# Layer 1's attention stream: another order of VectorE's and ScalarE's work in the slots, and the rows to route turned ahead of the tile's mixing

## The reference

```python
x = x + tanh(g_xattn[0]) * L0_xattn(layernorm(x), ctx)   # attention both ways, gated
x = x + tanh(g_ffn[0])   * L0_ffn(layernorm(x))          # 8 experts, the 4 best per token
x = x + tanh(g_xattn[1]) * L1_xattn(layernorm(x), ctx)
x = x + tanh(g_ffn[1])   * L1_ffn(layernorm(x))          # 8 experts, the 2 best per token
```

```python
queries, keys, values = x @ Wq.T + bq, ctx @ Wk.T + bk, ctx @ Wv.T + bv
attn = softmax(queries @ keys.T / 16)
out = (x + attn @ values) @ Wo.T + bo
gate_logits = y @ gate_w + gate_b           # y: layernorm of the stream after attention
topk_vals, topk_idx = top_k(gate_logits, 2)  # softmax over the two gives the weights
```

## Time and profile before

| what | us |
|---|---|
| median of three runs (1516.46 to 1520.41) | 1517.4 |
| the profiled execution's own time | 1517.85 |
| its span | 1516.0 |
| layer 0's attention and routing, 0 to about 500 | 500 |
| layer 0's experts, to about 927 | 427 |
| layer 1's attention stream, about 927 to 1220 | 293 |
| layer 1's last routing and experts, to the end | 296 |
| TensorE busy over the span | 1400.1 (92%) |
| VectorE busy | 790.1 (52%) |
| ScalarE busy | 736.8 (49%) |
| GpSimd busy | 504.6 (33%) |

### The profile page before, as it was taken

How to read it: one execution, slowest core, us unless ns; L and a number is a source line. 1 busy time by engine, 2 the same in 40 slices (tenths; PEclk the granted TensorE clock), 3 DMA queues, 4 the chain that set the end, 5 groups by cost and what they waited for, 6 DMA issues and landing times. The chain is left out here.

```text
span 1516.0 us, 25943 instructions
## 1 busy us (share of the span) xinstructions
PE 1400.1 (92%) x10086; PEld 1281.0 (84%) x10086; DVE 790.1 (52%) x1658; ACT 736.8 (49%) x1399; POOL 504.6 (33%) x389
## 2 busy tenths in 40 slices
PE   5799989999998999999999999999989889999997
PEld 5686966967855899999999898998979769899996
DVE  3545666666656353554454233465665775455421
ACT  3344454454443465555565454454442435666653
POOL 1200100101011664665565443131211125667643
PEclk8899999999999999999999999999998979999999
DMA  4302022021113453553553234031202145555332
GB/s 135 126 12 70 29 75 71 15 87 59 43 52 101 118 144 53 145 148 61 121 152 61 53 54 119 1 109 51 76 32 85 30 155 155 128 132 154 66 52 37
DMA packets 73680, 127.57 MB, mean 84 GB/s; under 512 B 7952, under 2 KB 53664, under 8 KB 73504
## 3 DMA queue, kind: packets, MB, share of 16 engines
q1 hardware_dynamic: 46816, 81.92, 16.4%
q0 software_dynamic: 26688, 43.34, 15.0%
HBM read 100.44 MB, written 24.79 MB: 83 GB/s over the span
## 5 line engine op out<-in xcount | busy, mean ns | idle before, releaser
L2425 DVE TENSOR_TENSOR m_hidden_lo<-m_act_out,m_hidden_hi 128x512 fp32r<-128x512 f32 x224 | 155.0, 692 | 363.2 <-ACT m_hidden_hi L2367 324.2
L420 PE MATMUL banks<-m_down_hi,m_hidden_hi 128*128 128x256 f32 x896 | 258.6, 289 | 4.1 <-DVE m_hidden_lo L2425 3.4
L420 PE MATMUL banks<-m_down_lo,m_hidden_hi 128*128 128x256 f32 x896 | 254.9, 284 | 2.9 <-issue 2.9
L420 PE MATMUL banks<-m_down_hi,m_hidden_lo 128*128 128x256 f32 x896 | 254.8, 284 | 0.0
L420 PE MATMUL banks<-m_xt_hi,m_up_hi 128*128 128x256 f32 x640 | 185.6, 290 | 3.3 <-DVE m_xt_lo L2408 3.3
L420 PE MATMUL banks<-m_xt_hi,m_up_lo 128*128 128x256 f32 x640 | 182.0, 284 | 0.0
L420 PE MATMUL banks<-m_xt_lo,m_up_hi 128*128 128x256 f32 x640 | 182.0, 284 | 0.0
L420 PEld LDWEIGHTS banks<-m_down_hi,m_hidden_hi 128*128 128x128 f32 x896 | 171.1, 191 | 8.9 <-DVE m_hidden_lo L2425 4.9
L420 PEld LDWEIGHTS banks<-m_down_lo,m_hidden_hi 128*128 128x128 f32 x896 | 171.2, 191 | 3.3 <-issue 3.3
L420 PEld LDWEIGHTS banks<-m_down_hi,m_hidden_lo 128*128 128x128 f32 x896 | 171.0, 191 | 0.0
L2504 POOL DMA_INDIRECT m_other_block<-rows,list_i x84 | 91.3, 1087 | 162.8 <-DVE list_i L1495 99.7
(11 more groups left out here) (367 smaller groups left out, 3568.5 us busy)
## 6 DMA issues: line engine op xcount, KB each, us to landing
stage<-in_down SPq DMA_DIRECT2D x22, 512.0 KB
stage<-in_ctx_cols SPq DMA_DIRECT2D x26, 402.0 KB
stage<-in_ctx_rows SPq DMA_DIRECT2D x20, 512.0 KB
stage<-in_up SPq DMA_DIRECT2D x20, 512.0 KB
m_stage<-in_up SPq DMA_DIRECT2D x11, 512.0 KB
m_stage<-in_down SPq DMA_DIRECT2D x10, 512.0 KB
rows<-xn SPq DMA_DIRECT2D x8, 528.0 KB, 3.4
stage<-in_ctx_picked SPq DMA_DIRECT2D x8, 512.0 KB
```

The costliest lines, as they stand in the source:

```text
L420: mm = q.e.matmul(dst, a, b, start=first and n == 0, stop=last and n == 2, skip_group_check=True)
L2425: q.e.tensor_tensor(lo, m.act[(n * HP + h) % ACTS], f32(hi), ALU.subtract).then_inc(*hidden_lo.mark((layer, n, h)))
```

## The change

It has five parts, all in layer 1's stream.

1. `who`: the low parts of the context's columns of batches 1 to 3 all go to DVE (two more pieces of 128x804 in slots 3, 7 and 11; POOL does two fewer). Rows are split as before.
2. `vector_attention_1`: the statistics of batch b+2 (`norm_in`) move from the end of slot i = 3 to slot i = 2, ahead of the queries' low parts. The two marks of slot i = 2 move to the next slot, ahead of `vector_scores`. In slot i = 3 the two puts stand ahead of the columns.
3. `mix_first`: in slots 8, 9, 12, 13, 16 and 17 `turned_lo` stands ahead of `vector_scores`.
4. TensorE turns the rows to route ahead of the mixing in slots 6, 10 and 14. ScalarE makes xn at the start of these slots, right behind the probabilities' high parts, and `a_routed_hi` ahead of `a_mixed`.
5. `vector_place` is cut in two; in the last batch its first instruction, which reads the bank, stands at the end of slot 16 and not in slot 17.

```diff
@@ who
-                return ("a", "pd"[n[2] % 2]) if n[0] else ("a", "d")
+                return ("a", "p" if kind == "cr" and n[2] % 2 == 0 else "d") if n[0] else ("a", "d")
@@ tensor_attention_1
+                if b and i == 2:
+                    tensor_turn_x(q, "r", 1, b - 1)
                 if 1 <= t <= LAST:
                     tensor_mix(q, 1, *of_tile(t - 1))
-                if b and i == 2:
-                    tensor_turn_x(q, "r", 1, b - 1)
@@ scalar_attention_1
                 if 1 <= t <= LAST:
                     scalar_turn_probs(q, 1, *of_tile(t - 1))
+                if b and i == 2:
+                    scalar_apply(q, "out", 1, b - 1)
...
-                elif i == 2:
-                    if b:
-                        scalar_apply(q, "out", 1, b - 1)
-                    if more:
-                        scalar_queries(q, 1, b + 1)
+                elif i == 2 and more:
+                    scalar_queries(q, 1, b + 1)
...
+                if b and i == 2:
+                    scalar_turn_x(q, "r", 1, b - 1)
                 if 1 <= t <= LAST:
                     scalar_mix(q, 1, *of_tile(t - 1))
...
-                if b and i == 2:
-                    scalar_turn_x(q, "r", 1, b - 1)
@@ vector_attention_1
+                if 2 <= b < BATCH and i == 3:
+                    vector_mark(q, 1, b - 2, 0)
+                    vector_mark(q, 1, b - 2, 1)
+
+                mix_first = b >= 2 and i < 2
+                if mix_first:
+                    vector_turn_mix(q, 1, *of_tile(t - 2))
                 if t < LAST:
                     vector_scores(q, 1, b, i)
-                if t >= 2:
+                if t >= 2 and not mix_first:
                     vector_turn_mix(q, 1, *of_tile(t - 2))
...
-                        vector_place(q, 1, b - 2)
+                        vector_place_parts(q, 1, b - 2)
...
                 elif i == 2:
+                    if b + 2 < BATCH:
+                        vector_measure(q, "in", 1, b + 2)
                     if more:
                         vector_queries(q, 1, b + 1)
-                    if b >= 2:
-                        vector_mark(q, 1, b - 2, 0)
-                        vector_mark(q, 1, b - 2, 1)
                 elif i == 3:
                     if more:
                         vector_bias(q, 1, b + 1)
-                        convert(q, "d", columns_of(b + 1))
                     if b >= 2:
                         vector_put(q, 1, b - 2, 0)
                         vector_put(q, 1, b - 2, 1)
+                    convert(q, "d", columns_of(b + 1))
+                    if b >= 2:
                         vector_mark(q, 1, b - 2, 2)
                         vector_mark(q, 1, b - 2, 3)
-                    if b + 2 < BATCH:
-                        vector_measure(q, "in", 1, b + 2)
...
                 if t == LAST:
                     vector_weigh(q, 1, b - 2)
+                    vector_place_number(q, 1, b - 2)
```

6 lines of the change are left out of this document (5 added, 1 removed).

## The result

| | us |
|---|---|
| before, median of 4 runs (1516.43 to 1520.41) | 1516.9 |
| after, median of 4 runs (1488.21 to 1495.64) | 1491.5 |
| ratio, with its 95% interval | 0.983 [0.980, 0.986] |
| the profiled execution of after; its span | 1495.64; 1493.8 |
| forecast; its range | 1499.0; 1491 to 1511 |

What follows compares the result with a forecast made beforehand. TensorE sets the pace, so its waits and its clock in layer 1's stream can be won: 9.7 us of waits plus 8.75 of clock, 18.45, give 1499.4 us (1499.0 against the median), range 1491 to 1511.

Steps and rivals of the forecast that it cites:

- reaches the end: The question whether the stream's gain reaches the kernel's end; behind the stream the experts are TensorE's too.
- The sum of waits: TensorE's waits in layer 1's stream, summed over slots: 9.7 us won.
- tail, slots 4 and 8: TensorE's waits for the low part of the probabilities' tail, 1.9 us twice, both go: +3.8 us.
- slot 6: Routed rows' turning: the wait of 1.28 us gives way to a new bank wait of 2.6 us: -1.3 us.
- slot 10: Routed rows' turning ahead of the mixing: a wait of 3.67 us becomes 2.6 us: +1.1 us.
- slot 14: No queries here, the bank comes free with the probabilities' low parts and xn is ready in time: +2.0 us.
- slot 9: The output's gain from an earlier `turned_lo` is given back at VectorE's first `a_x`: 0 us.
- bank wait at the second half of L684: Slots 6 and 10: TensorE waits 2.6 us for a bank that `a_cols_lo` of the queries' first half frees.
- rival (d): Slower: the columns on VectorE stay at 2.4 us each, the kernel takes 1524 us; chance 0.06.
- The clock: Falls of TensorE's clock behind waits that go are won back: 8.75 us, bounds -1.7 to 13.9.
- Rival (b): The clock comes back in full, no new fall: 23.6 us won, 1494.3; chance 0.16 shared with another rival.
- rival (a): The clock doesn't come back, falls stay where tiny products and a short wait meet: 8.0 us, 1509.9; chance 0.18.

Runs made afterwards that it cites:

- e1: The kernel before with parts 1 and 2 alone (columns' low parts all on VectorE, statistics, marks and puts moved): ratio 0.987 to before.
- e5: The changed kernel without part 4, the routed rows turned behind the mixing again: ratio 0.985 to before, stream 237.4 us.
- e10: The changed kernel measured once more with no further edit, in another set: ratio 0.983 to before, median 1488.3 us.
- e2: The kernel before with part 4 alone, the routed rows turned ahead of the mixing: ratio 0.996 to before.
- e3: The kernel before with part 3 alone, `turned_lo` ahead of the greatest score in slots 8, 9, 12 and 13: ratio 0.995 to before.
- e4: The kernel before with idle products ahead of slot 12's choosing and slot 13's output, no work moved: ratio 0.997 to before.
- e6: The changed kernel without part 3, `turned_lo` behind the greatest score again: ratio 0.989 to before.
- e7: The changed kernel with half of the columns' low parts back on GpSimd: ratio 0.989 to before.
- e12: The changed kernel with queries' high parts ahead of the exponential (slots 6, 10), plus reorderings around slots 5, 9, 13, 14 and 17: ratio 0.981 to before.
- e9: The kernel before with idle products at seven places of slots 4 to 14 where TensorE waited, no work moved: ratio 0.999 to before.

## Why the prediction was right or wrong

**What bounds the kernel: right.** TensorE's waits and its clock, in the stream, are where the 25.2 us come from, and behind the stream the time is the same. That isn't quite the forecast's "reaches the end": TensorE stands 3.2 us longer there, and the clock happens to lose 3.8 less. Of the 25.2 us 0.9 are slot 1's fall, which is chance.

**The sum of waits, 9.7 forecast, was about right.** By the profile it is 11.4 in the stream; 1.6 of it are given back behind the stream's end, which leaves 9.8. By the average of the remainder it is 12.1 (3.0). Point by point, from the earlier trace rows and their answers:

| term | forecast | measured |
|---|---|---|
| tail, slots 4 and 8 | +3.8 | 1.89 + 1.87 to 0: +3.8 |
| lists | +0.9 | 0.92 to 0.24: +0.7 |
| slot 6 | -1.3 | 1.28 to 2.23: -0.95 |
| slot 10 | +1.1 | 3.67 to 2.22: +1.45 |
| slot 14 | +2.0 | 1.49 + 0.49 to 0.90: +1.1 |
| slot 13 | +1.3 | 2.52 to 0.97: +1.55 |
| slot 9 | 0 | 2.53 to 0.98 + 1.06: +0.5 |
| slot 12 | +1.7 | 2.15 to under 0.3: +1.9 |
| place | +0.2 | 1.51 gone, L1547 for `a_x` 0.45 to 2.01: -0.05 |

The bank wait at the second half of L684 exists, at the place named, and is 2.2 and not 2.6 us. TensorE, ScalarE and VectorE in after, slot 6:

```profile
1030.94 0.60 PE L684 MATMUL banks<-small,xn 128*128 128x128 f32 x4
```

```profile
1032.15 0.20 ACT L927 ACTIVATION_READ_ACCUMULATOR a_probs<-banks,nbias 128x1 f32 x1
```

```profile
1032.96 1.41 DVE L557 SCALAR_TENSOR_TENSOR a_cols_lo<-banks,fold_cols,a_cols_hi 128x512 fp32r<-128x512 f32 x2 [0.24 <-ACT a_cols_hi L550]
```

The exponential ends at 1032.35, 0.8 us behind the first four transposes (forecast 0.96), and the bank is free 1.4 us later, at 1033.77 (forecast 1.65). The columns' 0.99 us held, so rival (d) didn't come. That `xn` would be ready in slot 14 was wrong by 0.9 us. Slot 9's gain did come back at `a_x` as the prediction says, but not quite all.

**One term had the right size under the wrong name.** Slot 10 was booked on part 4. e1 shows that moving the marks takes the wait from 3.67 to 1.28, with the turning where it was, and e5 that with the other parts in part 4 wins nothing measurable. Terms of a sum that meet at one wait can't be added without asking what the wait is once the other part is in.

**The clock, 8.75 forecast, is the step that failed.** It gave 13.9 by TensorE's busy time and 13.5 (3.0) on average over the runs, the upper bound of the prediction's range (13.9). Of the whole miss of 7 us this is about 5; the rest is the waits' term (12.1 on average against 9.7). The step that failed reads: half of 3.55 comes back in slot 10, a new fall of 1.7 in slot 6, and one more of that size. In the profiles of after and e10 all 3.55 came back and slot 6 has no fall. The one more did come, as slot 16's fall of 6.8 us instead of 3.4, but slot 1's fall of the same size was gone by chance, so that the sum is 10.35 + 3.55 - 1.7 + 1.7 = 13.9. That it meets the bound exactly is luck. Rival (b) came nearest, at 1494.3 still 3 us above what was measured. The reason that I gave against it was the 2.6 us of standing in slots 6 and 10. The Trainium skill, "TensorE: Matmul & The Clock Gate", section "Part 1: The HAM clock gate", says that the throttled state is the default and that activity releases it. The prediction read from it that the whole 13.9 comes back, and set it aside; the sum agrees with that reading, slot 16's fall in every profile doesn't.

**Why that reason didn't hold** is partly open. The profiles that have the same wait show how often a fall comes with it (it begins at most 0.7 us ahead of the wait's end and 2.7 behind it, in the last two rows up to 4.5). Tiny products are those of 16 columns or fewer for choosing, lists and key bias:

| wait of TensorE | in profiles of | waits | with a fall |
|---|---|---|---|
| probabilities, 2.2 us, slot 1, ahead of every edit | all | 14 | 2 |
| tail, 1.9 us, slot 4 | before, e2, e3, e4 | 4 | 3 |
| routed rows, 3.7 us, slot 10 | before, e3, e4 | 3 | 3 |
| lists, 2.5 us, slot 11 | e2 | 1 | 0 |
| output, 2.5 us, slot 13 | before, e1, e2, e6 | 4 | 2 |
| output, 2.5 us, slot 9 | before, e1, e2, e4, e6 | 5 | 1 |
| L684, 2.2 us, slots 6 and 10 | after, e2, e6, e7, e10 | 10 | 2 |
| 1.0 to 1.5 us, slots 6, 9, 10, 13 and 14 | all but e2, e6 and e12 | 34 | 0 |
| tail, 1.9 us, slot 8, just ahead of 16 tiny products | before, e2, e3, e4 | 4 | 4 |
| choice, 2.1 us, slot 12, amid 32 tiny products | before, e1, e2, e6 | 4 | 4 |
| 0.6 us, slot 11, amid 32 tiny products | all | 14 | 9 |
| tail, 1.7 us, slot 12, ahead of 32 tiny products | e7 | 1 | 1 |
| 1.0 us, slot 16, just ahead of 32 tiny products | all | 14 | 14 |

The length of a wait alone doesn't tell. Of the 38 waits of 1.9 to 2.5 us with no tiny products beside them 10 have a fall, of the 23 waits of 1.0 to 2.1 us with tiny products beside them all have one, the shortest too. Slot 16 in after, as an example:

```profile
1171.83 0.44 PE L1010 MATMUL banks<-small,a_mixed 128*128 128x128 f32 x2 [1.04 <-DVE a_probs_t_lo L555]
```

The tiny products alone don't tell either: in slots 8 and 12, where the wait beside them was brought to 0.6 us or less by moving work, one of 16 has a fall (e3, slot 12). So the runs speak for the two together, a wait and tiny products beside it, but by counting; no experiment moved the tiny products. This is what the prediction lacked: its 2.6 us in slots 6 and 10 have none beside them, while the falls that parts 1 to 3 took away in slots 8 and 12 do. Slot 12 has 32 of them (lists and choice), not the 16 that its rival (a) counted. Slot 9's 2.53 us without a fall was the one row on a wait outside the places that fell, and I took it as the exception. The prediction also put the 1.8 us of 1115 to 1135 on slot 10's wait; that fall lies in slot 11, 10 us later, and comes with slot 10's wait at 1.28 us too (e1, e5). It is missing in the five profiles that have the 2.2 us at L684 in slot 10 (after, e2, e6, e7, e10) and there in the nine others; why is open. That standing has a part in the falls is shown by e4 and e9, where only idle products were added and 7.6 and 11.4 us of the clock came back. That something beside the instructions has one too is shown by slot 1, where the same instructions with the same wait have a fall in 2 of 14 profiles; whether it is the moment at which a wait comes was not tried.

**The parts overlap.** Alone, parts 1 and 2 shorten the stream by 17.6 us, part 4 by 7.0 and part 3 by 7.6, together 32.2; the change shortens it by 25.2. Slot 1's fall, which of these five profiles only that of before has, is in each figure with 0.9 us, so without it 29.5 stand against 24.3. The overlap is in part 4, whose gain alone was the clock's, behind a wait that part 2 shortens anyway.

## What to carry to other kernels

Read what the clock loses behind waits as a term of its own, and ask of each fall at which place it lies and what TensorE does there: here the remainder, mostly waits, was worth 12 us and the clock that went with it 13, and each wait of 1 us or more with tiny products beside it had a fall. A cut in VectorE's work can come from taking the other half of it away from GpSimd, when both read SBUF at the same time: four pieces at 0.99 us were cheaper than two at 2.06 to 2.70. Where two parts of a change lean on one wait, cost the second with the first one in, and measure each alone and each left out.
